# Role adapter on Trainium2: batches sorted by four, with the down product's weights stationary

## What is computed

```python
# x: (64, 64, 512) = batches x rows x features; role: (64,), values 1 and 2
out = jnp.clip(x + cms_out + modifier, 0.0, 1.0)          # end of L0, all matmuls fp32

h = jnp.einsum('bsh,bhk->bsk', hidden_states, W_down[role]) + b_down[role][:, None, :]   # 512 -> 256
h = jax.nn.gelu(h, approximate=False)
u = jnp.einsum('bsk,bkh->bsh', h, W_up[role]) + b_up[role][:, None, :]                   # 256 -> 512
y = hidden_states + u
mean = jnp.mean(y, axis=-1, keepdims=True)
var = jnp.mean(jnp.square(y - mean), axis=-1, keepdims=True)
yn = (y - mean) * jax.lax.rsqrt(var + LN_EPS)
return yn * gamma[role][:, None, :] + beta[role][:, None, :]
```

## Time and profile before

| | us |
|---|---|
| three runs: median, lowest, highest | 2032.5, 2031.72, 2033.04 |
| the profiled execution | 2032.4 |
| its span, from first to last instruction | 2030.8 |
| adapter, from the first down bias matmul to the end of the span | 1895.4 to 2030.8 |
| last row tile (`yo`) written | 2022.3 |

### The profile page before, as it was taken

How to read it: one execution, slowest core, us unless ns; L and a number is a source line. 1 busy time by engine, 2 the same in 40 slices (tenths; PEclk the granted TensorE clock), 3 DMA queues, 4 the chain that set the end, 5 groups by cost and what they waited for, 6 DMA issues and landing times.

```text
span 2030.8 us, 28039 instructions
## 1 busy us (share of the span) xinstructions
PE 2005.9 (99%) x9371; PEld 1670.6 (82%) x9371; DVE 1391.9 (69%) x2601; ACT 950.2 (47%) x1977; POOL 107.4 (5%) x199
## 2 busy tenths in 40 slices
PE   8999999999999999999999999999999999999997
PEld 7888878888888888888888888888888888888896
DVE  6786786555777686556686786565686686654897
ACT  4754453433654454333564453343374454433564
POOL 0000000000000000000000000000000000000132
PEclk9999999999999999999999999999999999999999
DMA  4121233315111143125111232224311132222754
GB/s 167 32 63 42 75 123 109 94 52 202 63 52 63 52 145 109 50 90 206 65 53 48 68 116 97 89 94 152 118 35 60 53 114 99 94 74 75 247 162 116
DMA packets 113024, 193.79 MB, mean 95 GB/s; under 512 B 12393, under 2 KB 72050, under 8 KB 108404
## 3 DMA queue, kind: packets, MB, share of 16 engines
q1 hardware_dynamic: 98404, 128.42, 20.1%
q0 software_dynamic: 14400, 63.46, 8.9%
q10 hardware_dynamic: 80, 0.13, 0.0%
HBM read 148.71 MB, written 43.26 MB: 95 GB/s over the span
## 4 chain that ended last, share of the span: by engine, by line
PE 91%; DVE 5%; DMA 2%; issue 1%; SPq 1%; ACT 0%; DVEq 0%; POOL 0%; POOLq 0%
PE y L1712 16%; PE y L1714 15%; PE y L1713 15%; PE x L1712 13%; PE x L1714 13%; PE x L1713 13%; PE y L1801 1%; PE x L1826 1%; DVE w_lo L1145 1%; DMA bet<-beta 1%; DVE c_forms L1307 1%; DMA w_blocks<-w1m 1%; PE x L2062 1%; DVE f L1211 0%; PE y L1800 0%
## 5 line engine op out<-in xcount | busy, mean ns | idle before, releaser
L693 ACT CAST w_hi<-w_blocks 128x512 fp32r<-128x512 f32 (+1 forms) x464 | 231.4, 519 | 124.6 <-PE y L1714 83.7
L1145 DVE TENSOR_TENSOR w_lo<-w_blocks,w_hi 128x512 fp32r<-128x512 f32 (+1 forms) x464 | 249.9, 564 | 54.7 <-ACT w_hi L693 54.7
L1712 PE MATMUL x<-h_hi,w_hi 128*128 128x512 f32 x512 | 199.7, 390 | 0.0
L1712 PE MATMUL y<-h_hi,w_hi 128*128 128x512 f32 x512 | 199.4, 389 | 0.0
L1713 PE MATMUL x<-h_lo,w_hi 128*128 128x512 f32 x512 | 199.3, 389 | 0.0
L1713 PE MATMUL y<-h_lo,w_hi 128*128 128x512 f32 x512 | 199.2, 389 | 0.0
L1714 PE MATMUL y<-h_hi,w_lo 128*128 128x512 f32 x512 | 199.2, 389 | 0.0
L1714 PE MATMUL x<-h_hi,w_lo 128*128 128x512 f32 x512 | 199.2, 389 | 0.0
L1712 PE MATMUL y<-a_forms,w_hi 128*128 128x512 f32 x480 | 187.9, 391 | 2.1 <-DVE f L1248 2.0
L1714 PE MATMUL y<-a_forms,w_lo 128*128 128x512 f32 x480 | 186.9, 389 | 0.0
L1713 PE MATMUL y<-a_forms,w_hi 128*128 128x512 f32 x480 | 186.8, 389 | 0.0
(11 more groups left out here) (240 smaller groups left out, 4243.2 us busy)
## 6 DMA issues: line engine op xcount, KB each, us to landing
w_blocks<-w1m SPq DMA_DIRECT2D x128, 256.0 KB, 4.5
w_blocks<-w1c SPq DMA_DIRECT2D x64, 256.0 KB, 3.2
w_st<-w2c SPq DMA_DIRECT2D x64, 256.0 KB, 3.1
w_st<-w2m SPq DMA_DIRECT2D x64, 256.0 KB, 4.7
x_hi_lo<-x_halves POOLq DMA_DIRECT2D x6, 2048.0 KB, 11.0
zs<-z_by_batch SPq DMA_DIRECT2D x66, 128.0 KB, 2.1
cms<-f SPq DMA_DIRECT2D x32, 256.0 KB, 2.8
z_cms<-cms POOLq DMA_DIRECT2D x8, 1024.0 KB, 7.0
```

What stands on the lines that cost most here:

```text
L693: nc.scalar.copy(w1_hi[:, w % RING, cols], src).then_inc(w1_hi_s, 1)
L1145: nc.vector.tensor_tensor(w1_lo[:, w % RING, cols], src, f32(w1_hi[:, w % RING, cols]), ALU.subtract).then_inc(w1_lo_s, 1)
L1712: nc.tensor.matmul(ps, w[0], x[0], start=first, stop=False, skip_group_check=more)
```

## The change

- The sort now fills fours first: four batches of one role (two successive pairs, 256 rows) for pairs 4 to 27, that is fours q = 2 to 13 (`FOURS` = 14), where pairs 2q and 2q + 1 share one role. Pairs 0 to 3 and 28 to 32 are done as before (`PAIRED`). The links are 48 in place of 40 ahead of the gather, spread over the first four queries; `sort_gather` moves behind the seventh query, `sort_pairs` to the first step of the attention loop.
- For a four, the down product has the weights stationary (128x128 blocks out of a copy) and z moving, 256 columns for both pairs at once: 24 matmuls into two banks. The hidden so comes by feature, and needs no transpose. Its bias (`bdcol`) goes into gelu, which ACT runs twice on each bank: once for `ht_hi`, once for the fp32 value (`hs`), from which DVE makes `ht_lo` in one instruction of 512 columns.
- The copy: ACT issues a DMA of 1 MB from `wd_hi_lo` to `four_weights0` or `four_weights1` for each four (the role is known only at run time), two of them behind the first gelu, then one behind each four's gelu.
- Orders change: DVE does a four's rows in `rows_of_four`, SP issues loads in twos, and three small loads (`bdcol`) are added at the start.
- `z_hi`, `z_lo`, `hs`, `ht_hi` and `ht_lo` are twice as wide.

The diff, cut to its core:

```diff
+FIRST_Z = ((2,), (3, 4), (5, 6), (7,))
+FIRST_LOADS = ((6,), (7,), (8,), (9, 10), (11,))
+
+
+FIRST_LATE = 2 * (LATE // 4 - 2) + 1
+PAIRED = (*range(4), *range(2 * FOURS, NPAIR))
+
+SLOTS_KNOWN = 8 + 11 + 3 * R + 20
...
+                if n == FIRST_LATE:
+                    sp.wait_ge(last_stored[0], 16)
+                    sp.wait_ge(last_stored[1], 16)
                 batches_ = [batch_of(table, n) for table in (first_t, second_t)]
                 if n >= 4:
                     sp.wait_ge(zl_s, n - 3)
@@ -497,22 +540,20 @@
...
 
-            def unit(m, u, load):
-
-                if load:
-                    load_z(m + 6, (u + 2) % 4)
+            def unit(m, u):
+
+                for n in FIRST_LOADS[m] if m < 5 else (m + 7, m + 8) if m % 2 else ():
+                    if n < NPAIR:
+                        load_z(n, n % 4)
                 if m:
                     store_second(m - 1, u + UNROLL - 1)
 
             for m in range(NPAIR):
-                if m == 4 * UNROLL + 1:
-                    sp.wait_ge(last_stored[0], 16)
-                    sp.wait_ge(last_stored[1], 16)
-                unit(m, m, m + 6 < NPAIR)
+                unit(m, m)
                 if m == 4:
                     sp.wait_ge(z1_ready, DC * NS)
                     store_z(NT - 2, h2_tile, last_stored[0])
-                if m == 4 + 2 * DC:
...
-            inverse_std(0, 0)
-            for n in range(NPAIR - 1):
-                store_first(n, n)
-                inverse_std(n + 1, (n + 1) % 2)
+            for n in range(NPAIR):
+                if n in PAIRED:
+                    inverse_std(n, n % 2)
+                    if n < NPAIR - 1:
+                        store_first(n, n)
+                elif n % 2 == 0:
+                    for i in (n, n + 1):
+                        inverse_std(i, i % 2)
+                    for i in (n, n + 1):
+                        store_first(i, i)
             for u in range(UNROLL):
                 pool.wait_ge(a_stored[u], 16 * ((NPAIR - 2 - u) // UNROLL + 1))
...
+                if n >= 4:
+                    act.wait_ge(zt_s, n - 3)
                 for c in range(DC):
...
+            def gelu_four(q):
+
+                n = 2 * q
+                if q == 2:
+                    act.wait_ge(bd_loaded, 16 * R)
+                r = act.value_load(role_t[0:1, n:n + 1], min_val=0, max_val=R - 1)
+                for m in range(KD // P):
+                    cols = slice(m * 2 * P, (m + 1) * 2 * P)
+                    act.wait_ge(d_mm, n + m + 1)
+                    bias = bdcol[:, bass.ds(r, 1), m]
+                    nc.scalar.activation(ht_hi[:, hid(n), cols], four_bank(q, m), ACT.Gelu, bias=bias)
+                    nc.scalar.activation(hs[:, hid(n), cols], four_bank(q, m), ACT.Gelu, bias=bias).then_inc(ht_hi_s, 1)
+
+
+            def load_weights(q):
+
+                r = act.value_load(role_t[0:1, 2 * q:2 * q + 1], min_val=0, max_val=R - 1)
+                if q == 2:
+                    act.wait_ge(wd_lo_s, R)
+                    act.wait_ge(hlo_s, 8 * NQ * NS)
+                act.dma_start(f32(wf[q % 2][:]).rearrange("p h k n -> p (h k n)"),
+                              f32(wd_hl[:, bass.ds(r, 1)]).rearrange("p o h k n -> p (o h k n)")).then_inc(wf_in[q % 2], 16)
+
+            def gelu_next(n):
+                if n in PAIRED:
+                    gelu_pair(n)
+                else:
+                    gelu_four(n // 2)
+                    if n // 2 + 2 < FOURS:
+                        load_weights(n // 2 + 2)
+
+            gelu_pair(0)
+            load_weights(2)
+            load_weights(3)
+            for n in range(NPAIR):
+                if n in PAIRED:
+                    split_hidden(n)
+                    if n < 4:
+                        split_z(FIRST_Z[n][0], FIRST_Z[n][0])
+                    elif n == 2 * FOURS + 1:
+                        split_z(NPAIR - 1, NPAIR - 1)
+                    if n + 1 < NPAIR:
+                        gelu_next(n + 1)
+                    for i in FIRST_Z[n][1:] if n < 4 else ():
+                        split_z(i, i)
+                elif n % 2 == 0:
+                    split_z(n + 4, n + 4)
+                    split_z(n + 5, n + 5)
+                    gelu_next(n + 2)
 
             b = act.value_load(first_t[0:1, NPAIR - 1:NPAIR], min_val=0, max_val=B - 1)
             act.wait_ge(yo_s, NPAIR)
...
                     if s:
                         z1_clip(s - 1, c)
                     if s == 0 and c == 0:
+                        sort_ranks()
+                    if s == 0 and c == 2:
+                        sort_late()
+                    if s == 0 and c == 3:
...
                         z2_clip(s - 1, 2 * p)
                         z2_clip(s - 1, 2 * p + 1)
                     split_v(m + 1)
+                    if s == 0 and p == 0:
+                        sort_pairs()
                     if p in (3, 4):
...
+            def hidden_low_four(q):
+                n = 2 * q
+                dve.wait_ge(ht_hi_s, n + 2)
+                nc.vector.tensor_tensor(ht_lo[:, hid(n), :], hs[:, hid(n), :], f32(ht_hi[:, hid(n), :]),
+                                        ALU.subtract).then_inc(ht_lo_s, 2)
+
+
+            def rows_of_four(n, low):
+
+                r = role_of(n)
+                stats(n, n)
+                dve.wait_ge(st_s, n + 1)
+                moments(n, n % 2)
+                centre(n, n, r)
+                if low:
+                    split_z(n + 6, n + 6)
+                stats(n + 1, n + 1)
+                dve.wait_ge(st_s, n + 2)
+                moments(n + 1, (n + 1) % 2)
+                scale_shift(n, n, r, n + 1 > UNROLL)
+                centre(n + 1, n + 1, r)
+                if low:
+                    split_z(n + 7, n + 7)
+                scale_shift(n + 1, n + 1, r, n + 2 > UNROLL)
+
+            def rows_of_pair(n, low):
+
+                r = role_of(n)
+                stats(n, n)
+                dve.wait_ge(st_s, n + 1)
+                if n + 1 in PAIRED and n + 1 < NPAIR:
+                    hidden_low(n + 1)
+                moments(n, n % 2)
+                centre(n, n, r)
+                for i in low:
+                    split_z(i, i)
+                scale_shift(n, n, r, n + 1 > UNROLL)
+
+
+            def z_piece(n):
                 if n < 2:
                     z1_sum(s, n + 2)
                 elif n < 4:
@@ -1695,6 +1849,26 @@
...
+            split_z(2, 2)
+            z_piece(0)
+            for n in range(3):
+                rows_of_pair(n, FIRST_Z[n + 1])
+                z_piece(n + 1)
+            for q in range(2, FOURS):
+                n = 2 * q
+                hidden_low_four(q)
+                if q == 2:
+                    rows_of_pair(3, (8, 9))
+                else:
+                    rows_of_four(n - 2, True)
+                z_piece(n)
+                z_piece(n + 1)
+            hidden_low(2 * FOURS)
+            rows_of_four(2 * FOURS - 2, False)
+            for n in range(2 * FOURS, NPAIR - 1):
+                rows_of_pair(n, (NPAIR - 1,) if n == 2 * FOURS else ())
             last = NPAIR - 1
...
+            def down_four(q, between):
+
+                pe.wait_ge(zl_s, 2 * q + 2)
+                pe.wait_ge(wf_in[q % 2], 16 * (q // 2))
+                for m in range(KD // P):
+                    if m:
+                        between()
+                    for k in range(DC):
+                        w = halves(wf[q % 2], k, slice(m * P, (m + 1) * P))
+                        ins = mm3(four_bank(q, m), w, (z_hi[:, q % 2, k, :], z_lo[:, q % 2, k, :]), k == 0, k == DC - 1)
+                    ins.then_inc(d_mm, 1)
+
+            def turn_z(n):
...
-                if n + 1 < NPAIR:
-                    r_next = pair_role(n + 1)
-                turn(n, n)
-                if n + 1 < NPAIR:
-                    down(n + 1, n + 1, r_next)
-                up(n, n, r)
+                if n in PAIRED:
+                    if n + 1 < NPAIR:
+                        r_next = pair_role(n + 1)
+                    turn_hidden(n)
+                    turn_z(n)
+                    if n + 1 < NPAIR:
+                        down_next(n + 1, r_next, lambda: None)
+                    up(n, r)
+                elif n % 2 == 0:
+                    r_next = pair_role(n + 2)
+                    turn_z(n)
+                    down_next(n + 2, r_next, lambda: turn_z(n + 1))
+                    up(n, r)
+                    up(n + 1, r)
+                else:
+                    continue
                 r = r_next
-
-
 # ---- launch: one core; the host only lays arrays out ----
 def kernel(**inputs):
```

234 lines of the change are left out of this document (137 added, 97 removed).

## The result

The changed kernel takes 2069.6 us (median; its runs lie between 2063.0 and 2072.2), the kernel before 2032.6 beside it: 1.0176 times as long, 95% interval 1.0163 to 1.0189. The forecast was 2038. The profiled execution of after is its quickest, 2063.0 us with a span of 2061.4; it starts the adapter (the issue of beta, 1891.98 us) 1.6 us later than before. That difference can't be put down to the change alone: in the other runs of the changed kernel, whose L0 is the same, beta is issued between 1889.5 (half_copies) and 1895.3 us (kept_numbers). All else comes behind that.

The account below looks back on a forecast made before the run. The prediction held the adapter bound by TensorE and about equally by SP's last load. Start +4.0, one store fewer -1.6, end +3.0 and sort +0.1 made +5.5 on the profiled 2032.4: 2038 us, range 2027 to 2047.

Parts of the forecast that it names:

- The bound before: Adapter before the change: its end hangs on SP's last load about as much as on TensorE (3.59 us per pair).
- -1.6 for one store fewer: SP's queue: loads go in twos, so one store less stands ahead of z(32); -1.6 us (1.2 to 1.6).
- SP's work: SP's reads and issues in the adapter: none removed, 3.56 to 3.85 us per pair, 7.1 to 7.7 per four.
- The copies in the middle: 0: One 1 MB weight copy per four in the adapter: 0 us for waiting on it (bounds 0 and 12 x 2).
- rival 3: DMA congestion in the adapter's fours: longer tile-to-tile loop or late copies, +6 on top, 2044 us (2041 to 2050); chance 0.17.
- its loop: From an output tile through store, landing and load to four pairs later: 13.0 us for two fours, 17.7 with slow landings.
- share 0.94: DMA busy share in the adapter's middle with the copies: 0.56 + 0.38 = 0.94.
- the slow store: Beside a 1 MB store, POOL's store lands in 4.9 us instead of 2.3; used as evidence that queues share engines.
- The start: +4.0: Adapter's start: first two copies delay beta by 3.4 us, z_lo(4) ahead of first tile adds 0.6; +4.0 (0.6 to 5.9).
- The end: +3.0: Adapter's last pairs: one more round of rows behind z_lo(32), starting up to 0.6 us sooner; +3.0 us (2.7 to 3.6).
- TensorE's work and DVE: Adapter's fours: PE work falls 10.3 us, DVE is next at 6.56 us per four, so at most 7.4 can show.
- The sort: +0.1: Sort: PE gap of 0.43 us may close, sort_pairs makes PE's output product wait 0.5 to 0.6; +0.1 (-0.4 to +0.7).

Follow-up runs that it names:

- half_copies: Changed kernel with the ten later weight copies halved to the high halves (512 KB instead of 1 MB): 2057.4 us, 1.0123 times the kernel before.
- kept_numbers: Changed kernel, but SP keeps a pair's second batch number from load to store, two reads per pair instead of three: 2062.3 us, 1.0146 times before.
- before_kept: Kernel before, with SP keeping a pair's second batch number from load to store, two reads instead of three: 0.9998 times before, median 2033.0 us.
- no_copies: Changed kernel without any weight copy (all fours use role 0's down weights in place), SP keeping the second batch number: 2037.9 us, 1.0023 times before.
- pool_no_mid: Changed kernel with second-half output stores (but the last) moved from SP's to POOL's queue and the ten later weight copies left out: 2044.8 us, 1.0058.
- no_mid_copies: Changed kernel with only its first two weight copies, the ten later ones left out: 2047.9 us, 1.0073 times before.
- stores_on_pool: Changed kernel with all second-half output stores but the last moved from SP's queue to POOL's, all copies kept: 2054.4 us, 1.0102 times before.
- before_with_copies: Kernel before, with ACT also issuing ten 1 MB copies of down weights into two tiles nobody reads: 2048.9 us, 1.0081 times before.

## Why the prediction was wrong, point by point

**The bound before.** I held that the adapter's end hung on SP's last load as much as on TensorE, since ACT's last cast had waited 0.29 us for it. before_kept showed SP with 6.6 us of slack. A load that arrives just in time isn't what sets the end, when the queue that issues it is itself held back: SP's pace of 3.85 us per pair was TensorE's pace. The sums hung on it failed too. z(32) went out 111.2 us behind s(0) (2030.22 - 1919.05), forecast 95 to 97; ACT's cast of pair 32 waited for nothing, and from it to the end of the last tile it was 18.5 us, forecast 15. So the -1.6 for one store fewer ahead of z(32) isn't seen in any run.

**SP's work** is the step that failed most. "None is removed" and "3.56 to 3.85 us per pair" counted its instructions rightly and took their durations from a trace in which no such copies ran. They took 4.49 us per pair, so 9.0 per four instead of 7.1 to 7.7. Over the twenty pairs that is 12.9 us more than before: a read took 0.474 us instead of 0.311, a load's issue 0.487 instead of 0.376. With the ten copies left out they took 0.309 and 0.379 and the kernel was 21.7 us faster; with SP's stores moved to POOL and all copies in place it was 15.2 faster.

**The copies in the middle: 0.** The 0 was right for what it looked at, the wait for four_weights, which never came. What the copies do to others was put into rival 3 and given 0.17. Loads did land slower (3.5 us instead of 2.1), but with the measured medians (3.5, POOL's stores 2.5 instead of 2.3) its loop is 14.6 us, 7.3 per four, and would still hide behind SP's 7.7. SP waited for landed stores only once it had a read less to do (13.9 us in kept_numbers; 0.5 in after from 1925 us on). Its price, +6, was far too small, because it left SP's own slow steps out. It was also reckoned wrongly: two thirds of the way from 13.0 to 17.7 us is 16.1, 8.1 per four and not 8.3, which gives +4; and the loop passes 7.7 per four when its two landings average 1.2 us above the quiet ones, not 1.5. With my estimate of share 0.94 (the trace has about 0.8) the rows of the slow store should have been read for all who use the DMA engines and tables at that time. Together the ten copies cost 21.7 us.

**The start: +4.0.** Beta's delay was forecast as 3.4 and was 2.2, and it went when the copies came later (13.3 us to landing), so that mechanism was right. The Trainium skill's rule (DMA: Bandwidth & Descriptors, "Queues, rings and completion order"), round robin over the queues packet by packet, is in agreement with both numbers, as far as they show that transfers of a second queue, issued later, delay beta. The step that failed is the next one: I priced z_lo(4) ahead of the first tile as 0.6 us of DVE's time, and didn't ask when pair 4's load lands, which stands behind beta in the same queue. It cost 5.1 us more, and the first tile was 9.6 us late counted from the start of the span, 8.0 counted from beta's issue. By tile 4 it was 13.9 us, of which no_copies leaves 6.2 to the order itself.

**The end: +3.0.** There is no such term: tiles 28 to last take 12.6 us instead of 13.2 (14.2 in four of the other runs). That the extra round of a deeper pipeline is paid where it fills is my reading of what follows. By tile 4 DVE has made z_lo for three more pairs (1.8 us) and the statistics and ht_lo of one more (about 1.6), and in no_copies it idled some 2 us there that it hadn't before: together most of the 6.2 us.

**TensorE's work and DVE.** That TensorE's 10.3 us don't show, and that DVE at 6.56 us per four is next, was right: the undisturbed fours of pool_no_mid take 6.7.

**The sort: +0.1.** The gap of 0.43 us in TensorE did close (its timeline has none from 33 to 38 us), sort_pairs cost 0.7 (forecast 0.5 to 0.6), and a further 0.7 at about 55 us, where the gather on TensorE now stands, wasn't in the sum; its cause wasn't tested. Together +1.1 us at the 70th us.

**The sum.** After against before, profiled executions: start of the adapter +1.6, to tile 4 +13.9, tiles 4 to 28 +15.8, the end -0.6: +30.7 us, which is 2061.4 - 2030.8 but for rounding. By the medians the change cost 37.0 us, and no_copies, without any copy and with a read less on SP, has 31.7 of them back. The other runs of after are 5 to 9 us longer than the profiled one; where those us lie isn't in any trace. Rival 3 had the right disturbance, the copies' traffic, but the wrong path, and even its own range ended at 2050. The forecast's range left out its worse half; it should have reached to where every landing and every step of SP is slow.

## What to carry to other kernels

A copy that nobody waits for isn't free: price it at every small transfer, and at every read of a table and every issue by a sequencer, that runs beside it, and test the price by adding the bare copy to the kernel before. A queue that seems to tie with the busiest engine may only be following it; take a little work off it and see whether the end moves. When a tile is wanted one round earlier, look up what stands ahead of its load in the queue.

## What the runs showed of the hardware

A sequencer's read of one number gets slower beside other DMA traffic, and so does SP's issue of a load (0.487 us in after, 0.379 in no_mid_copies). Reads on ACT took 0.555 us on average with the copies and 0.301 without the ten (1940 to 2005 us), on SP 0.515 and 0.309. POOL's reads took 0.29 us in after too; with the stores on its queue they took 0.553 with the copies and 0.297 without, and its issues stayed at 0.54. The longest read was 1.65 us (stores_on_pool), the shortest in after 0.262. The Trainium skill (DMA: Bandwidth & Descriptors, "Latency and other measured facts") gives about 600 ns as the floor of such a read. The kernel after has a median of 278 ns for the reads of second_t, so here the measurement decides: the page's figure lies between the quiet read and a disturbed one.

TensorE's granted clock falls in stretches where it idles; in the kernel before it is 1.00 in every stretch from 1892 to 2008 us. From 1970 to 1990 us of after it is 0.83 on average. After 3.34 us of idle time the down product of a four starts at the lower level of 1.2 GHz: its matmuls follow each other at 0.21 us instead of 0.12. Timeline of PE, kernel after:
```profile
1979.51 0.58 PE L1886 MATMUL y<-z_hi,four_weights 128*128 128x256 f32 x1 [3.34 <-DVE z_lo L1719]
1979.89 0.41 PE L1887 MATMUL y<-z_lo,four_weights 128*128 128x256 f32 x1
1980.11 0.41 PE L1888 MATMUL y<-z_hi,four_weights 128*128 128x256 f32 x1
```
This lies on the way from z_lo over gelu to DVE's ht_lo, so late loads may cost twice. How much of the 21.7 us it is wasn't tested apart. The 15.4 us of before_with_copies hold nothing of it: there the granted clock is 1.00 all through the adapter up to 2030 us.
